# Second MLP and experts in groups of two middle-layer blocks in place of four

## The reference

```
# the MLP of the attention branch, hidden size 3072
h = layer_norm(x, ln2_w, ln2_b)
h = gelu(h @ fc1_w + fc1_b) @ fc2_w + fc2_b
x = x + h
...
# experts: 4 of them, hidden size 1536, the best 2 are used for all tokens
pooled = x.mean(axis=1);  top 2 of pooled @ router_w.T + router_b, gates by softmax
h = act_e(x @ w1[e] + b1[e]);  out = gate[e] * (h @ w2[e] + b2[e])
y = x + sum(out);  layer norm of y with ln_g, ln_b;  result added to x
```

## Time and profile before

| What | us |
|---|---|
| runs: median of 3 | 1955.73 |
| runs: lowest and highest | 1953.89 and 1957.2 |
| span of the profiled execution | 1953.0 |
| busy in the span: PE | 1900.2 |
| busy in the span: DVE | 1171.0 |
| busy in the span: ACT | 609.8 |
| busy in the span: POOL | 401.0 |

### The profile page before, as it was taken

The page is one execution under the profiler, slowest core; times in us unless marked ns, Lnnn a source line. Parts: engine busy times, 40 slices in busy tenths (PEclk is TensorE's granted clock), DMA queues, the critical chain, the costliest instruction groups (busy, mean ns, idle before and its releaser), DMA issues.

```text
span 1953.0 us, 28486 instructions
## 1 busy us (share of the span) xinstructions
PE 1900.2 (97%) x10981; PEld 1811.5 (93%) x10981; DVE 1171.0 (60%) x2102; ACT 609.8 (31%) x1182; POOL 401.0 (21%) x311
## 2 busy tenths in 40 slices
PE   7999999999899999999999999999999999999998
PEld 4677999999799999789999999999989999999998
DVE  8998678998894323778524435254557435274348
ACT  6533238787784412225200001010330101010013
POOL 1000002210001222214413314043023404043130
PEclk9999999999899999999999999999989999999999
DMA  6332402121245110033201102020231102021014
GB/s 177 112 119 86 116 14 57 43 60 54 68 139 144 57 49 9 17 103 112 65 9 57 46 20 59 7 65 17 80 97 49 50 17 73 1 81 40 26 50 125
DMA packets 80943, 125.53 MB, mean 64 GB/s; under 512 B 7334, under 2 KB 51656, under 8 KB 80814
## 3 DMA queue, kind: packets, MB, share of 16 engines
q1 hardware_dynamic: 76254, 110.47, 19.5%
q10 hardware_dynamic: 4560, 13.31, 2.3%
HBM read 98.30 MB, written 25.45 MB: 63 GB/s over the span
## 4 chain that ended last, share of the span: by engine, by line
PE 86%; DVE 6%; ACT 5%; issue 3%; ACTq 0%; DVEq 0%; SPq 0%; DMA 0%
PE pb L1135 25%; PE pa L679 25%; PE pb L679 10%; PE pa L745 5%; PE pa L891 3%; PE pb L811 3%; PE pb L1044 3%; PE pa L845 3%; PE pb L891 2%; ACT sm L1557 1%; PE pb L687 1%; PE pb L922 1%; ACT o1h L1583 1%; PE pa L1006 1%; DVE sm L2146 1%
## 5 line engine op out<-in xcount | busy, mean ns | idle before, releaser
L1813 ACT ACTIVATE tr<-pb,V 128x418 f32<-128x418 f32 (+1 forms) x144 | 87.6, 610 | 765.9 <-PE pb L1135 752.9
L1135 PE MATMUL pb<-X_hi,uw_hi 128*128 128x416 f32 (+1 forms) x864 | 305.5, 354 | 2.4 <-DVE uw_lo L2464 2.4
L1135 PE MATMUL pb<-X_hi,uw_lo 128*128 128x416 f32 (+1 forms) x864 | 304.9, 353 | 0.0
L1135 PE MATMUL pb<-X_lo,uw_hi 128*128 128x416 f32 (+1 forms) x864 | 304.8, 353 | 0.0
L679 PE MATMUL pa<-dw_hi,hh 128*125 128x384 f32 x960 | 246.9, 338 | 1.0 <-ACT tr L1813 0.7
L679 PE MATMUL pa<-dw_hi,hl 128*125 128x384 f32 x960 | 246.3, 338 | 0.0
L679 PE MATMUL pa<-dw_lo,hh 128*125 128x384 f32 x960 | 246.1, 337 | 0.0
L2411 DVE CAST hh<-tr 128x418 fp32r<-128x418 f32 (+1 forms) x144 | 115.0, 799 | 202.4 <-ACT tr L1813 202.4
L1289 POOL CAST uw_hi<-raw 128x768 fp32r<-128x768 f32 x47 | 42.7, 908 | 715.4 <-PE pb L1135 618.3
L679 PEld LDWEIGHTS pa<-dw_hi,hh 128*125 128x125 f32 x960 | 172.4, 186 | 2.0 <-ACT tr L1813 1.0
L679 PEld LDWEIGHTS pa<-dw_hi,hl 128*125 128x125 f32 x960 | 173.1, 186 | 0.0
(11 more groups left out here) (418 smaller groups left out, 3517.1 us busy)
## 6 DMA issues: line engine op xcount, KB each, us to landing
raw<-in_L_mix_fc_w SPq DMA_DIRECT2D x48, 384.0 KB, 3.3
raw<-in_L_ffn_w SPq DMA_DIRECT2D x47, 384.0 KB, 3.2
md<-md_d SPq DMA_DIRECT2D x11, 546.9 KB
md_d<-mds SPq DMA_DIRECT2D x10, 546.9 KB
raw<-in_L_mix_qkv_w SPq DMA_DIRECT2D x24, 192.0 KB, 4.3
md<-md_d ACTq DMA_DIRECT2D x8, 546.9 KB
TOK<-in_x SPq DMA_DIRECT2D x10, 336.0 KB
xn_d<-TOK SPq DMA_DIRECT2D x10, 336.0 KB
```

Of the source, the lines that this page charges most:

```text
L1135: last = nc.tensor.matmul(pb[:, j % 4, 0:n], w_[:, kk, :], x_[:, kk, o:o + n], start=(kk == 0 and q == 0), stop=(kk == KT - 1 and q == 2))
L1813: last = A_(RE[f"tr{j % 3}"][:, 0:w], pb[:, j % 4, 0:w], ACT.Identity if func == "mish" else func, bias=bias(b))
```

## The change

GK becomes 2, and the numbers of groups double to 12 and 6 (24 groups in all). The order of the first group's jobs, the waits of the down tiles for the hidden values, the buffers and the hooks are fitted to it. The number of matmuls does not change: 24 groups of two blocks are the same 48 blocks as 12 groups of four.

```diff
-GK = 4
+GK = 2
-MLP_GROUPS, EXP_GROUPS = 6, 3
+MLP_GROUPS, EXP_GROUPS = 12, 6
...
     if group == 0:
-        return [(b, c) for c in range(NCH) for b in range(GK - 1)] + [(GK - 1, c) for c in range(NCH)]
+        return [(b, c) for c in range(NCH) for b in range(GK)]
     return [(b, c) for b in range(GK) for c in range(NCH)]
...
+def hidden_of(group, c):
+
+    return JOBS * group + max(n for n, (b, c_) in enumerate(up_order(group)) if c_ <= c) + 1
...
             for b in range(3):
                 graph_in(b)
-                block_page(up_page(0, b), fc1[:, :, b * P:(b + 1) * P])
+                if b < GK:
+                    block_page(up_page(0, b), fc1[:, :, b * P:(b + 1) * P])
                 tile_in(3 + b)
-            block_page(up_page(0, 3), fc1[:, :, 3 * P:4 * P])
...
-                pe.wait_ge(*at("h_lo", JOBS * group + JOBS - NCH + chunk_of(t) + 1))
+                pe.wait_ge(*at("h_lo", hidden_of(group, chunk_of(t))))
...
                 if n == 1:
                     tile_back(NT - 1)
                     pe.wait_ge(*at("l_ev", NT - 1))
-                if n == 2:
                     pe.wait_ge(*at("l_x", 7))
-                if n == 5:
+                if n == 3:
                     pe.wait_ge(*at("l_x", NT))
...
             for b in range(3):
-                up_split(0, b)
+                if b < GK:
+                    up_split(0, b)
                 tile_bias(4 + b)
...
-            up_split(0, 3)
...
                     if n == 1:
                         dve.wait_ge(*at("b2_in", 32 * (e + 1)))
-                    if 2 <= n < 2 + NT:
-                        t = n - 2
+                    for t in range(2 * n - 2, 2 * n) if n else ():
```

More of the change, by code:

```diff
@@ L315, in gps_layer @@
                   + [("pb_row", [TP, D], fp32)],
-                  [(f"h{k}{b}", [P, N], f32r) for b, k in ((0, "h"), (0, "l"), (1, "h"), (1, "l"), (2, "h"), (2, "l"), (3, "h"))])
+                  [(f"h{k}{b}", [P, N], f32r) for b in range(GK) for k in ("h", "l")])
         RW = area(pages("wu", range(KT)),
@@ L323, in gps_layer @@
                   pages("kv1", range(KT)), pages("wp", range(KT)),
-                  [("hl3", [P, N], f32r)] + pages("dw", range(GK)) + [(f"b2r{e}", [TP, D], fp32) for e in range(TOPK)])
+                  pages("dw", range(GK)) + [(f"b2r{e}", [TP, D], fp32) for e in range(TOPK)])
         RE = area([("c0w", [P, D], fp32), ("c0", [TP, D], fp32), ("a1", [TP, 2, D], fp32), ("bu", [TP, D], fp32),
@@ L348, in gps_layer @@
         wbp, uw = page_list(RE, "wb", H2), page_list(RE, "uw", 3)
-        hb_hi = [RM["hh0"], RM["hh1"], RM["hh2"], RM["hh3"]]
-        hb_lo = [RM["hl0"], RM["hl1"], RM["hl2"], RW["hl3"]]
+        hb_hi = [RM[f"hh{b}"] for b in range(GK)]
+        hb_lo = [RM[f"hl{b}"] for b in range(GK)]
         sm = [RW[f"sm{q}"] for q in range(3)]
```

## The result

| | before | changed |
|---|---|---|
| median of the runs beside each other, us | 1954.81 | 1998.49 |
| range of those runs, us | 1953.85 to 1957.2 | 1997.65 to 1999.56 |
| profiled execution, its span, us | 1953.0 | 1996.1 |
| first up job of the MLP to the end of the span, us | 1028.2 | 1068.6 |

The ratio is 1.0221, 95% interval 1.0207 to 1.0234: 2.2% slower, where 1993.1 us was forecast. On the spans it is +43.1 us against a sum of +37.4.

The account below looks back on a forecast made before the run. PE bounds the dense groups and sets the middle stage's pace with little to spare, DVE the last stage. Terms 21.0 + 9.4 + 6 + 1 = +37.4 give a span of 1990.4, median 1993.1 us; range 1979 to 2008.

Parts of the forecast that it names:

- Last stage: After PE's last up phase: 21.0 us of matmuls leave, DVE keeps the stage at 50.5 us, so +21.0 us.
- Rival A: Last and middle stages: PE sets them, so they shorten by what leaves; no change or 1962.7 us; chance 0.06.
- Middle stage: Between MLP and expert 1: 21.0 us of matmuls leave, 11.6 come back at a pitch of 4.05, so +9.4 us.
- the circle: Middle stage loop of addition, normalisation, transposes, matmuls, addition two tiles on: 8.1 us per two tiles, pitch 4.05.
- Expert 1's first group: Start of expert 1: PE waits 4.3 us at tile 2 for DVE, then half clock costs +1.7; together +6 us.
- Expert 2's first group: Start of expert 2: slot free at 25.7 us, PE wants it at 24.7; +1 us, bounds 0 and +6.
- Dense groups: Phases where PE alone sets the pace: 0 us; at worst 6 us for 120 more tile joints.
- Rival C: Middle stage: PE's clock falls to 1.2 GHz, stage +19 and expert 1's start +12, 2005 us; chance 0.2.
- Rival B: Dense groups: DVE late beside POOL in every group, 1 us lost in each of 21, 2014 us; chance 0.08.
- The port pair: Expert 1's first group: GpSimd and two-input VectorE instructions take turns, 2.12 against 0.59 us; the rule's full +13 not taken.

Follow-up runs that it names:

- e5: Kernel before with only its last group, at the end of expert 2, cut into two of two blocks: 1974.95 us, 1.0089 of the kernel before.
- e3: Groups of two as in the changed kernel, but of four blocks at the end of expert 2: 1970.32 us, 1.0094 of the kernel before.
- e8: Groups of two as in the changed kernel, but of four blocks first in each expert: 1988.07 us, 1.0156 of the kernel before.
- e4: Kernel before with groups of two only in dense stretches, four kept at MLP ends, expert starts and the end: 1955.84 us, ratio 1.0001.
- e9: The changed kernel's groups of two, in the buffers of the kernel before: 1990.25 us, 1.0196 of the kernel before.
- e7: Kernel before with MLP groups of 4, 4, 3, 3, 2, 2, 1, 1, 4 blocks, experts unchanged: 1960.95 us, ratio 1.0027.
- e2: Groups of two as in the changed kernel, but of four blocks at the end of the MLP: 1984.16 us, 1.0144 of the kernel before.
- e6: Kernel before with only the last MLP group cut into two of two blocks: 1969.10 us, 1.0065 of the kernel before.

## Why the prediction was right, and where it was off

The forecast of 1993.1 us was 5.4 low, on the spans 5.7: the four terms that it summed came out 1.4 lower together (36.0), and two that it had at nothing came out at 4.4 and 2.8.

- **Last stage, +21.0: right** (+20.3; e5 alone +21.4, e3 gives it back). The stage took 49.5 to 50.5 us in every kernel, whether 21, 31.5 or 42 us of matmuls lay in it. Rival A is excluded by that.
- **Middle stage, +9.4: right** (+8.5), and the pitch of 4.05 was 4.07 (28.47 us for the last seven tiles); the stage, 48.6 us, lies just under the 49 to 51 that was named as the sign. One reading was wrong, that PE set the pace before: the pairs there came every 10.28 us, the circle's 6.1 + 4.2, in which PE waited 0.35 us for ACT, and the same circle set it. Of what leaves a tile the stage gives back half, since the circle spans two tiles: from the first to the tenth addition it took 35.64 us (1411.53 to 1447.17) in place of 45.01, 9.4 less. The start gave 2.5 more (2.1 forecast), the tail 0.7 (none forecast).
- **Expert 1's first group, +6: right** (+5.9). The slot was to come free 31.7 us behind the first up job and did (1488.73 - 1457.01); PE had no more work from 27.9 (27.4 forecast), so it waited 3.85 in place of 4.3 (4 to 6 was named as the sign), and the first 36 matmuls took 9.25 us, not 8.50. That the slot's time came out to the tenth is in part luck: DVE started its first job 0.8 us later after the first up job than before and took 2.9 us for it, not 2.5, and the second job took 0.9, not 2.0. The half clock behind the wait came too: 0.64 was granted from 1488 to 1492. e8 removes the term.
- **Expert 2's first group, +1: right** (+1.3, of which PE waits 1.01 for the slot at tile 2).
- **Dense groups, 0: missed by 4.4.** That no wait comes up was right (e4: no change in the median with seven more groups; 21.06 + 20.52 us leaves 0.06 a pair, which are the joints). But the down phases of the changed kernel take 21.21 us, 0.15 more each, and 21.06 with the buffers of the kernel before (e9). The diff shows that buffers move; I put no price on it. The upper bound of 6 us that I gave for joints covers it by luck of size, not by mechanism.
- **Ahead of the change, 2.8 us, not in the sum.** First up jobs started between 921.6 and 929.4 in all profiles, and e7 (922.2) and e5 (929.4) have the same instructions up to there. The windows show why, first the kernel before, then the changed one:

```profile
846.00:850.00 4.00, 4.00 (x15) 3.77 (x14) 3.97 (x3) 1.80 (x2) 4.00 (x3) 0.58 0.79 167
850.00:854.00 4.00, 4.00 (x25) 4.00 (x24) 3.63 (x6) 0.00 (x0) 0.24 (x1) 1.00 0.00 0
```

```profile
846.00:850.00 4.00, 4.00 (x12) 2.99 (x11) 3.96 (x3) 1.55 (x2) 4.00 (x3) 0.50 1.07 232
850.00:854.00 4.00, 4.00 (x14) 4.00 (x14) 3.86 (x6) 0.25 (x1) 1.73 (x1) 0.50 0.09 22
```

Half clock (its lower level, 1.2 GHz) lasts longer in the second. Medians share this scatter, which is why totals of e2, e3 and e5 lie some us off the sums of their stages.
- **Rival C** had 0.2. The changed kernel kept 1.00 through the stage's tiles, so the forecast held; it was the likelier of two outcomes, and no reading of the forecast told them apart. In e6, e8 and their repeats C came, in a milder form: 55 us, at 0.61 to 1.00 granted by stretches of 4 us, not a stage at half clock throughout, so +6.4 and not the 9.6 between +9.4 and +19. The rule that the prediction cited (the Trainium skill, TensorE: Matmul & The Clock Gate, "HAM oscillation — how this bites in real kernels"), the low clock coming back again and again behind pauses, describes those four traces, four separate stretches behind pauses of 2.1 to 2.5 us; in the changed kernel one pause of 2.10 us and eight of 0.9 to 1.3 us brought no low clock. The section's own case has waits of 3 to 5 us, so "by that rule C is the outcome" took it further than it goes.
- **Rival B** is excluded for two and three blocks in dense groups, and is what e7 shows for one.
- **The port pair** (the Trainium skill, SBUF — State Buffer, "Who interferes with whom"): low halves of 2.12 us at 1471.76 beside POOL and 0.59 at 1474.20 without it. Only the first job of expert 1 met it; the forecast had given the second one a part of it too.

No kernel that was run beats the one before; e4 equals it.

## What to carry to other kernels

Smaller groups cost next to nothing where one engine does all the pacing, and cost up to their full share where a group's matmuls were the free filling of a stage that another engine or a circle of waits sets: look at the stages at the joints, and price the work that leaves them at its full time. Where a stage is a circle over two buffers, count the circle and not the busiest engine: cutting work of one tile moves the pitch by half of it. In dense places a group may shrink until its tile is as short as the consumer's work on it: here two blocks (2.1 us a tile) cost nothing, one (1.05 us) came at 1.22 us a tile.

## What the runs showed of the hardware

- The same instructions behind the same 2.08 us pause of PE ran at full or at half clock (48.6 or 55 us for one stage), the same way in each of the three kernels that were profiled twice. Where the clock fell, later pauses were 2.4 to 2.5 us and it fell again behind each; where it did not, they were 0.9 to 1.3 us.
- Identical code ahead of the MLP ended up to 7.2 us apart (922.2 in e7, 929.4 in e5; 921.6 to 929.4 over all kernels), with longer or shorter stretches of half clock.
- A down phase of 120 matmuls took 21.21 us in the changed kernel and 21.06 in e9, with the same instruction count (28846) and order of PE; the kernels differ in where buffers lie. 3.3 us in all.
